# A conditioned sequence model on one core: the set-up rebuilt, LayerNorm statistics in other forms, and five engine orders laid out anew

## The reference, cut to what matters

```python
xn = (x - mean(x)) * rsqrt(var(x) + eps)        # LayerNorm, then gain and bias where the layer has them
xm = xn * (1 + scale[seq]) + shift[seq]         # modulation from the conditioning vector of the sequence
x  = x + gate[seq] * (block(xm) + out_bias)
```

## Time and profile before

| | us |
|---|---|
| median of 3 runs | 629.04 (628.34 to 631.07) |
| profiled execution, its own time | 627.14 |
| its span, first to last instruction | 625.3 |
| PE busy | 524.5 (84%) |
| DVE busy | 463.3 (74%) |
| ACT busy | 350.3 (56%) |
| POOL busy | 328.0 (52%) |

### The profile page before, as it was taken

The page is one execution under the profiler, slowest core; times in us unless marked ns, Lnnn a source line. Parts: engine busy times, 40 slices in busy tenths (PEclk is TensorE's granted clock), DMA queues, the critical chain, the costliest instruction groups (busy, mean ns, idle before and its releaser), DMA issues.

```text
span 625.3 us, 24101 instructions
## 1 busy us (share of the span) xinstructions
PE 524.5 (84%) x10598; PEld 357.3 (57%) x10598; DVE 463.3 (74%) x1031; ACT 350.3 (56%) x576; POOL 328.0 (52%) x324
## 2 busy tenths in 40 slices
PE   2287886778799997878898998999889989988897
PEld 1154555645567674646656664666657655665675
DVE  7988677788878738766787497588995857689930
ACT  1037452233579667665674666436456976867842
POOL 4406110333546888764673452234537689856573
PEclk9999788787799996978999998598979999979999
DMA  8610353012315305124443421321232243032421
GB/s 299 248 27 18 72 157 77 22 41 56 90 35 156 121 16 150 52 58 127 145 106 99 127 74 44 92 73 42 92 105 69 65 125 102 22 114 61 124 68 68
DMA packets 35256, 56.91 MB, mean 91 GB/s; under 512 B 14672, under 2 KB 19664, under 8 KB 35152
## 3 DMA queue, kind: packets, MB, share of 16 engines
q1 hardware_dynamic: 34688, 54.42, 30.2%
q10 hardware_dynamic: 432, 0.94, 0.4%
q0 software_dynamic: 32, 0.01, 0.3%
HBM read 42.37 MB, written 3.54 MB: 73 GB/s over the span
## 4 chain that ended last, share of the span: by engine, by line
PE 43%; DVE 22%; POOL 16%; issue 12%; ACT 5%; DMA 1%; POOLq 0%; DVEq 0%
PE work L1059 8%; PE work L1010 7%; PE work L1025 6%; POOL x L650 4%; DVE stats L882 4%; PE work L967 3%; PE work L1002 3%; POOL rstd L641 3%; PE work L1068 3%; POOL xm L655 3%; PE work L970 2%; PE work L1038 2%; POOL x L646 2%; PE work L975 2%; DVE mx L850 2%
## 5 line engine op out<-in xcount | busy, mean ns | idle before, releaser
L722 ACT ACTIVATE xn<-x,nmr,rstd 128x128 f32<-128x128 f32 x192 | 78.3, 483 | 39.7 <-POOL nmr L643 39.7
L850 DVE TENSOR_REDUCE mx<-work 128x32 f32<-128x1024 f32 (+1 forms) x64 | 65.0, 1016 | 43.6 <-PE work L1010 41.5
L1059 PE MATMUL work<-xm,w_layer 128*128 128x512 f32 x176 | 95.2, 652 | 2.4 <-POOL xm L655 1.6
L1068 PEld LDWEIGHTS work<-w_layer,prob 128*128 128x128 f32 x704 | 81.7, 192 | 10.8 <-issue 5.6
L1010 PE MATMUL work<-kbd,q_gate 32*32 32x80 f32 (+1 forms) x4096 | 77.7, 273 | 11.8 <-issue 5.6
L650 POOL TENSOR_TENSOR x<-x,q_gate 128x512 f32<-128x512 f32 x48 | 60.7, 1270 | 49.7 <-DVE q_gate L899 48.5
L1068 PE MATMUL work<-w_layer,prob 128*128 128x128 f32 x704 | 84.7, 277 | 2.3 <-ACT prob L727 1.3
L655 POOL TENSOR_TENSOR xm<-turned_in,mod 128x512 f32<-128x512 f32 x48 | 50.6, 1055 | 66.0 <-DVE turned_in L894 65.9
L1010 PEld LDWEIGHTS work<-kbd,q_gate 32*32 32x32 f32 x4096 | 66.7, 112 | 28.0 <-issue 13.7
L713 ACT ACTIVATE prob<-prob 128x640 f32<-128x640 f32 (+1 forms) x64 | 56.5, 895 | 42.2 <-DVE prob L852 41.9
L727 ACT ACTIVATE prob<-work,first 128x512 f32<-128x512 f32 x88 | 58.6, 685 | 35.4 <-PE work L1059 34.9
(11 more groups left out here) (124 smaller groups left out, 804.3 us busy)
## 6 DMA issues: line engine op xcount, KB each, us to landing
q_gate<-gates_out SPq DMA_DIRECT2D x192, 128.0 KB, 2.8
vbd<-v_ev SPq DMA_DIRECT2D x128, 72.0 KB, 2.5
kbd<-in_adj SPq DMA_DIRECT2D x8, 704.0 KB, 6.6
edge_rep<-spread SPq DMA_DIRECT2D x32, 80.0 KB, 2.3
turned_in<-in_x_tok SPq DMA_DIRECT2D x8, 256.0 KB, 3.2
out_x<-x SPq DMA_DIRECT2D x8, 256.0 KB, 2.0
turned_in<-in_x_feat SPq DMA_DIRECT2D x7, 256.0 KB, 4.3
w_layer<-in_weights SPq DMA_DIRECT2D x2, 768.0 KB, 14.3
```

The lines of the kernel that those rows point to most:

```text
L722: act.activation(xn[s][:, t], x[s][:, t], ACT.Identity, scale=rstd[s][:, t:t + 1], bias=nmr[s][:, t:t + 1]).then_inc(xn_ready[s], 1)
L850: dve.tensor_reduce(mx[s][:], src, AX_X, ALU.max).then_inc(dve_step[s], 1)
L1059: pe.matmul(bank(s, f"h{j}.{u}"), w[UP[j]][:, 0, u * D:(u + 1) * D], xm[s][:], start=True, stop=True).then_inc(filled[s], 1)
L1068: last = pe.matmul(bank(s, f"y{a}")[:, t * D:(t + 1) * D], hT[s][u][:, t * P:(t + 1) * P], w[DOWN[a]][:, u], start=(u == 0 and t == 0), st ...
```

## The change

Four things are done.

1. The set-up. The modulation weights are loaded into `w_layer[2]` and `w_layer[3]`, the gates are built in `w_layer[1]`, and `silu` in a part of `q_gate`, so that no stream's buffers but these parts of `q_gate` are borrowed; the layers' own weights are loaded later (`weights` stages on SP: layers 2 and 3 once PE has finished the set-up, layer 1 once the gates are stored). SP waits for `first` before it loads chunk 1, and for the adjacency of chunk 0 before it loads the modulation weights. ACT now makes scale and shift out of PSUM (two activations a block), and only for the four blocks with a gain does DVE add one operation. ACT also does all eight clears. POOL clears nothing.
2. The adjacency of chunk 0 is not cast and multiplied by POOL: DVE reduces the integers and multiplies them itself.
3. The statistics: `bn_aggr` of a tile waits for its own `bn_stats` only, the small `memset` is gone, `neg_mean` is a `tensor_reduce` with negation, and adding epsilon has become a POOL operation in front of `rstd`.
4. All five `MERGE` strings are new. (`WARM` is an empty dictionary: `keep_warm` issues nothing.)

```diff
-CLEARS = [("clear", n, 0) for n in range(2 * NS - 1)]
+CLEARS = [("clear", n, 0) for n in range(3, 2 * NS)]
+SILU = [("silu", 0, 0)]
-SETUP = {"tensor": MODS + GATES, "vector": CLEARS + MODS + GATES, "scalar": GATES[1:], "gpsimd": [],
-         "sync": [("gates", 0, 0)]}
+SETUP = {"tensor": MODS + GATES, "vector": SILU + [MODS[j] for j in GAINED] + GATES, "scalar": SILU + CLEARS + MODS + GATES[1:],
+         "gpsimd": [], "sync": [("weights", 0, 0), ("gates", 0, 0), ("weights", 1, 0)]}
...
-    "vector": ("444004414414440444441332232003031330111202022031030030103031302311323101301010230130302223023221
+    "vector": ("010011244444240401001313020310100010001311231301231213321303330031330123012110302330312321233210
...
+            def clear(n):
+                tile = prob[n // 2][:, :, :, NONGT:] if n % 2 == 0 else vbd[n // 2][:]
+                flat = tile.rearrange("p g q m -> p (g q) m") if n % 2 == 0 else tile.rearrange("p t h v -> p (t h v)")
...
+                act.activation(flat, zeros.broadcast_to(shape), ACT.Copy).then_inc(act_clear, 1)
...
+                    if a in GAINED:
+                        act.activation(scale, ps[:, 0:B], ACT.Identity, scale=vec("gain", k), bias=gained_scale[:, k:k + 1])
+                        act.activation(shift, ps[:, B:2 * B], ACT.Identity, bias=gained_shift[:, k:k + 1]).then_inc(mod_ready, 1)
...
+                    dve.scalar_tensor_tensor(out=shift, in0=mod_bank[a][:, 0:B], scalar=vec("gain_bias", k), in1=shift,
+                                             op0=ALU.mult, op1=ALU.add).then_inc(gain_ready, 1)
...
-                    pool.wait_ge(veps_ready[s], count(c, NBLK, a + 1))
+                    pool.wait_ge(dve_step[s], count(c, OWN_STEPS, OWN["aggr", a]))
+                    pool.tensor_tensor(veps[s][:], mv[s][:, :, 1], eps[EPS[a]][:], ALU.add).then_inc(pool_step[s], 1)
+                    pool.wait_ge(pool_step[s], count(c, 4 * NBLK, 4 * a + 1))
                     pool.tensor_tensor(rstd[s][:], veps[s][:], neg_half[:], ALU.pow).then_inc(pool_step[s], 1)
...
-                    own(("stats", a))
-                    dve.memset(wait_slot[:], 0.0)
                     for t in range(T):
+                        dve.wait_ge(dve_step[s], count(c, OWN_STEPS, OWN["stats", a] - T + t + 1))
                         dve.bn_aggr(mv[s][:, t], stats[s][:, t]).then_inc(dve_step[s], 1)
                     own(("aggr", a))
-                    dve.tensor_scalar(neg_mean[s][:], mv[s][:, :, 0], -1.0, None, ALU.mult)
-                    dve.tensor_scalar(veps[s][:], mv[s][:, :, 1], EPS[a], None, ALU.add).then_inc(veps_ready[s], 1)
+                    dve.tensor_reduce(neg_mean[s][:], mv[s][:, :, 0:1], AX_X, ALU.add, negate=True).then_inc(mean_ready[s], 1)
```

More of the change, by code:

```diff
@@ L139, with runs @@
 MODS = [("mod", n, 0) for n in range(NBLK)]
-CLEARS = [("clear", n, 0) for n in range(2 * NS - 1)]
+CLEARS = [("clear", n, 0) for n in range(3, 2 * NS)]
+SILU = [("silu", 0, 0)]
 GATES = [("gates", n, 0) for n in range(2)]
-SETUP = {"tensor": MODS + GATES, "vector": CLEARS + MODS + GATES, "scalar": GATES[1:], "gpsimd": [],
-         "sync": [("gates", 0, 0)]}
+SETUP = {"tensor": MODS + GATES, "vector": SILU + [MODS[j] for j in GAINED] + GATES, "scalar": SILU + CLEARS + MODS + GATES[1:],
+         "gpsimd": [], "sync": [("weights", 0, 0), ("gates", 0, 0), ("weights", 1, 0)]}
 def lanes(engine):
-    streams = [[st for c in range(s, NCH, NS) for st in chunk_stages(c) if st[0] in PARTS[engine]] for s in range(NS)]
+    def runs(st):
+        return st[0] in PARTS[engine] and not (engine == "gpsimd" and st[0] == "edges" and st[2] in EDGE_DVE)
+    streams = [[st for c in range(s, NCH, NS) for st in chunk_stages(c) if runs(st)] for s in range(NS)]
     return streams + [SETUP[engine]]
@@ L276, in build @@
         neg_half = sb("neg_half", [P, T])
-        wait_slot = sb("wait_slot", [P, 1])
+        eps = {value: sb(f"eps_{k}", [P, T]) for k, value in enumerate(sorted(set(EPS)))}
         zero_col = sb("zero_col", [P, 1])
@@ L472, in width, with await_mod, adj_count @@
             return NONGT if a < 2 else S
+        def await_mod(eng, j):
+            eng.wait_ge(mod_ready, j + 1)
+            eng.wait_ge(gain_ready, sum(g <= j for g in GAINED))
+        def adj_count(c, k):
+            return sum(2 for b in range(c % NS, c, NS) if b not in EDGE_DVE) + k
         def modw(j):
@@ L599, in _ @@
             pool.memset(neg_half[:], -0.5)
+            for value, tile in eps.items():
+                pool.memset(tile[:], value)
             pool.memset(zero_col[:], 0.0).then_inc(const_step, 1)
@@ L675, in stage @@
                 s = c % NS
+                if kind == "clear":
+                    clear(a)
+                if kind == "silu":
+                    act.activation(sig, pair_cond, ACT.Exp, scale=-1.0).then_inc(cond_step, 1)
+                if kind == "mod":
+                    ps, k = mod_bank[a], MOD_COL[a]
+                    act.wait_ge(setup_filled, BEFORE_MODS + 1 + a)
+                    scale, shift = mod[:, 2 * a], mod[:, 2 * a + 1]
+                    if a in GAINED:
+                        act.activation(scale, ps[:, 0:B], ACT.Identity, scale=vec("gain", k), bias=gained_scale[:, k:k + 1])
+                        act.activation(shift, ps[:, B:2 * B], ACT.Identity, bias=gained_shift[:, k:k + 1]).then_inc(mod_ready, 1)
+                    else:
+                        act.activation(scale, ps[:, 0:B], ACT.Identity, bias=scale_bias[:, k:k + 1])
+                        act.activation(shift, ps[:, B:2 * B], ACT.Identity, bias=vec("shift_bias", k)).then_inc(mod_ready, 1)
                 if kind == "gates":
@@ L907, in _, with keep_warm @@
         def _(pe):
-            pe.wait_ge(const_step, 1)
+            def keep_warm(to, kind):
+                for _ in range(WARM.get(kind, 0)):
+                    pe.matmul(to, ident16[:], ident16[:].unsqueeze(1).broadcast_to([P, T, P]), start=True, stop=True)
+            pe.wait_ge(const_step, CONSTS)
+            pe.wait_ge(masks_step, HEAD_MASKS)
+            keep_warm(mod_bank[1], "start")
             pe.wait_ge(first_loaded, 16)
@@ L981, in stage @@
                     n = width(a)
+                    warm = ("graph scores" if a < 2 else "scores") + f" {pair}"
+                    if WARM.get(warm):
+                        await_bank(pe, c, f"S{pair} a{a}")
+                        keep_warm(work[s][:, 0], warm)
                     if pair == 0:
@@ L1033, in stage @@
                 if kind == "norm":
+                    if WARM.get("norm"):
+                        await_bank(pe, c, f"xn{a}")
+                        keep_warm(bank(s, f"xn{a}"), "norm")
                     for t in range(T):
                         pe.wait_ge(xn_ready[s], count(c, T * NBLK, T * a + t + 1))
-                        if t == 0:
+                        if t == 0 and not WARM.get("norm"):
                             await_bank(pe, c, f"xn{a}")
```

260 lines of the change are left out of this document (147 added, 113 removed), and 6 rows, old and new, of the table VECTORS.

## The result

The changed kernel takes 591.25 us in the median of 4 runs (585.31 to 594.09), against 628.69 of before in the same comparison (620.24 to 631.07): ratio 0.943, 95% interval 0.931 to 0.956. I had forecast 615, range 602 to 627. The direction held, the size did not: -37 us where -14 was forecast. The profiled execution was the fastest of its four: own time 585.31, span 583.5, granted clock 0.950, where the other three had 0.930 to 0.936. Its trace therefore shows some 6 us more of a gain than the median does.

What follows compares the result with a forecast made beforehand. A start set by DVE, a loose stretch to 180 us, then PE nearly full were taken to bound the kernel. 627.1 - 9 (start) - 2.3 (statistics) - 3 (orders) + 2.5 (end) = 615.3, given as 615, range 602 to 627.

Steps and rivals of the forecast that it cites:

- The start, -13.4 and +4.4 left for later: Set-up: first scores at 42 us against 55.43 (-13.4), work left for later costs +4.4; worth -9, between -4.4 and -13.4.
- Statistics, -2.3: 48 LayerNorm statistics places: 20 us less DVE work, fewer stalls, epsilon addition moved to POOL; -2.3, bounds -9 and +8.
- the +8 bound: Slow end of the statistics term: most of POOL's 13 us of added work exposed, stalls moved to other operations.
- the slower rival: MLP stretches: POOL becomes the bound as its 48 longer statistics stages are exposed (+13); 638 us, chance 0.10.
- The port: Start: DVE operations with two SBUF inputs may stall beside POOL; three stalls of 1.3 us would cost 4 us.
- The orders between 42 and 600 us, -3, bounds -12 and +8: New stage orders after the start: streams run further apart, winning part of PE's 69.7 us idle time; -3.
- The much faster rival: 55 to 180 us: wider stream spacing cuts PE's idle 26.8 us to 13, less work at 1.2 GHz; about 600, chance 0.14.
- The end, +2.5: Last two norm stages: no down stage behind them hides the modulation, so PE waits; +2.5, between 0 and 5.
- Time comes back: Rival, no change: work left behind and a poorer interleave eat the earlier start; 628 us, chance 0.11.
- set-up no faster: Rival at the start: ACT's clears or SP's waiting loads run late, scores start at 50; 623 us, chance 0.15.

Runs made afterwards that it cites:

- the long row at 1.2 GHz: Changed kernel with 1024 more products of the values kind in one unbroken row behind its last stage, result not used; the row lasts 26 us.

## Why the prediction was off

- **The start, -13.4 and +4.4 left for later.** Right in mechanism and size where it was read: 9.9 us of lead at 5% of the work. First scores at 38.5. ACT's clears took 2.12 us (2.1 forecast), the integer multiplication on DVE 1.61 (1.5 to 3.0). It is worth 3 to 7 us at the end of the program, depending on the orders; I had -9 as the value, so it was over-sized by 2 to 6. One reading beside it was loose: a third of POOL's 3.0 us is 1.0 and does not lie close to the reduction's 1.6, which was the right neighbour.
- **Statistics, -2.3.** Measured -2 and -5, neither clearly apart from nothing. POOL's exposure, the +8 bound and the slower rival's mechanism, is not seen in the time: POOL still waits 27.3 us for the variances, within the 25 to 35 forecast. But it waits in 20 places and not in 40, so that the addition stands behind other work of POOL in 28, where I had counted eight.
- **The port.** L878, with two inputs in SBUF, takes 0.35 us while POOL is idle and 1.06 us while POOL works (17.92 and 24.88 in the rows above; POOL's cast runs from 23.14 to 25.79); over the program its eight take 0.35 to 1.55. L865 ran with POOL idle and was not stalled, so of the 4 us that I allowed for three such operations hardly one came. By the Trainium skill (GPSIMD Engine Reference, Key points), DVE instructions with two SBUF inputs contend with GpSimd; the trace agrees.
- **The orders between 42 and 600 us, -3, bounds -12 and +8. This is the step that failed**: -23 alone, -30 in the changed code. I sized it by PE's idle time (69.7 us) and a guess at what could be won of it, and put PE's busy time at a constant. The runs show the reverse: the orders took 19 to 32 us out of PE's busy time, as less work at 1.2 GHz, and 5 to 8 out of its idle time. The sign was in the profile of before and not in the sum. Its mean clock of 0.915 is 106 us at 1.2 GHz, half of it lost to PE and hidden in its busy time, so "90% busy" was not full. And issue had a large share of the chain of before:

```profile
PE 43%; DVE 22%; POOL 16%; issue 12%; ACT 5%; DMA 1%; POOLq 0%; DVEq 0%
```

  PE's own waits put down to issue are 29 us; I never asked what they were. They are halved, though longer waits for DVE take most of that back. The much faster rival named the clock and the spacing of the streams, at 600 and 0.14; it confined them to the stretch of 55 to 180 us. There PE's idle time fell from 26.8 to 19.1 us (13 in the rival) and the clock rose from 0.82 to 0.86, while most of the gain came behind it. That the spacing of the streams is what raises the clock was not tested.
- **The end, +2.5.** PE waits 0.48 us: DVE and POOL do one chunk's modulation while PE still transposes the other, in a `norm` pair of 2.03 us. Inside its bounds, mis-sized by 2.
- **The rivals.** Time comes back, slower and set-up no faster did not happen. Much faster came nearest, 9 us above the measured time, by a mechanism of which the clock is borne out, in too small a place.

## What to carry to other kernels

TensorE's idle time is no bound for what a new order can win: half of its time at 1.2 GHz stands in its busy time. Look too at its pauses put down to issue inside runs of many small products. Both change with the order, and both can be read from one profile; but fewer pauses of one kind can come back as waits of another, so compare the sum of the idle time too. Joined halves of two sets of orders lost 3 to 18 us at the seam, even where TensorE's own positions nearly agreed.

## What the hardware showed that I had not expected

- TensorE's instructions come in pieces of 16 KB, 128 products with their loads. In the long row at 1.2 GHz one came each 3.47 us, 27 ns a product, where the products themselves took 16.8; in the kernels pieces start 3.3 us apart at the least.
- The same program got clocks from 0.879 to 0.934 in 53 runs of before, and its span went with it, from 637 to 618 us, loosely (correlation 0.69).
- A DVE multiplication with an integer operand of 1408 elements takes 1.61 us, as the reduction does.
